# Key-major attention of one Trainium2 kernel: the turn of the maxima placed behind a two-head look in the memory stage, and the transfers of the rows of maxima issued by ScalarE instead of SyncE

## Time and profile before

| | |
|---|---|
| runs of the kernel before | 4800.02, 4809.53, 4809.84 us; median 4809.53 |
| the profiled execution | 4812.54 us |
| its span, first to last instruction | 4810.8 us, 75801 instructions |
| busy, share of the span | PE 80%, VectorE 71%, ScalarE 50%, GpSimd 30% |
| memory attention, looks and steps | about 3190 to 3575 us of the span |
| cross-self attention, looks and steps | about 3950 to 4665 us of the span |

### The profile page before, as it was taken

One profiled execution on the slowest core, in us unless ns is written; L12 is line 12 of the kernel. 1 busy time (PEld: TensorE's weight loads), 2 busy tenths in 40 slices (PEclk: granted clock), 3 DMA queues, 4 the chain that ended last, 5 costly groups with the idle time before them and its releaser, 6 DMA issues. The chain is left out here.

```text
span 4810.8 us, 75801 instructions
## 1 busy us (share of the span) xinstructions
PE 3834.0 (80%) x28914; PEld 2206.9 (46%) x28979; DVE 3405.1 (71%) x5269; ACT 2397.4 (50%) x3237; POOL 1425.0 (30%) x1078
## 2 busy tenths in 40 slices
PE   4740988999999999999984838849985858888883
PEld 3630445666666666666652514424433422222231
DVE  6469675878777877878774246667754658888868
ACT  2120224666666666666652125526652437767772
POOL 0000432666666666666663250000000000000000
PEclk5565998999999999999995659969986869999996
DMA  0010840000000000000002164145520433323300
GB/s 20 1 55 0 191 117 28 1 15 15 1 15 1 15 1 15 1 15 1 1 1 97 39 158 56 30 77 84 85 36 22 94 77 51 50 42 53 50 2 9
DMA packets 155463, 194.79 MB, mean 40 GB/s; under 512 B 23685, under 2 KB 117502, under 8 KB 154468
## 3 DMA queue, kind: packets, MB, share of 16 engines
q1 hardware_dynamic: 144068, 167.17, 17.3%
q0 software_dynamic: 9856, 22.67, 1.8%
q10 hardware_dynamic: 1184, 0.12, 0.0%
HBM read 145.03 MB, written 42.42 MB: 39 GB/s over the span
## 5 line engine op out<-in xcount | busy, mean ns | idle before, releaser
L3121 POOL TENSOR_TENSOR arena<-arena 128x512 f32<-128x512 f32 (+1 forms) x768 | 1133.2, 1477 | 629.9 <-ACT arena L3075 575.7
L2568 ACT ACTIVATE arena<-ps 128x1024 f32<-128x1024 f32 (+1 forms) x688 | 703.2, 1023 | 332.5 <-PE ps L2493 321.9
L2586 DVE TENSOR_REDUCE arena<-ps 128x2 f32<-128x826 f32 (+1 forms) x576 | 564.8, 981 | 182.2 <-PE ps L2439 173.9
L3137 DVE TENSOR_TENSOR arena<-arena 128x1024 f32<-128x1024 f32 (+1 forms) x448 | 653.2, 1497 | 34.9 <-ACT arena L3104 34.9
L3159 DVE TENSOR_TENSOR arena<-ps,arena 128x512 f32<-128x512 f32 (+1 forms) x768 | 530.3, 691 | 108.8 <-ACT arena L3069 75.3
L2439 PE MATMUL ps<-arena 48*128 48x413 bf16 (+3 forms) x1920 | 437.0, 334 | 133.8 <-DVE arena L2586 66.8
L3069 ACT ACTIVATE arena<-ps 128x1024 f32<-128x1024 f32 (+1 forms) x448 | 410.5, 960 | 200.6 <-PE ps L2997 194.8
L3075 ACT ACTIVATE arena<-arena 128x1024 f32<-128x1024 f32 (+1 forms) x448 | 425.0, 992 | 60.4 <-DVE arena L3137 57.9
L2512 PE MATMUL ps<-arena 128*9 128x256 f32 (+2 forms) x5504 | 437.1, 390 | 10.3 <-ACT arena L2556 7.5
L2997 PE MATMUL ps<-arena 64*128 64x256 f32 (+1 forms) x3328 | 427.4, 391 | 5.9 <-ACT arena L3091 1.3
L3011 PE MATMUL ps<-arena 128*64 128x256 f32 (+1 forms) x3328 | 411.1, 387 | 6.4 <-ACT arena L3075 6.4
(11 more groups left out here) (661 smaller groups left out, 5357.4 us busy)
## 6 DMA issues: line engine op xcount, KB each, us to landing
arena<-ctx_parts SPq DMA_DIRECT2D x96, 200.1 KB
arena<-ctx_parts SPq DMA_DIRECT2D x192, 100.1 KB
arena<-fs_rows SPq DMA_DIRECT2D x128, 128.0 KB, 6.7
arena<-in_ctx_feat SPq DMA_DIRECT2D x8, 1601.0 KB, 6.4
arena<-in_ctx SPq DMA_DIRECT2D x16, 768.0 KB
arena<-diff_att_stack SPq DMA_DIRECT2D x60, 192.0 KB, 6.6
ctx_parts<-arena SPq DMA_DIRECT2D x24, 400.2 KB, 7.4
arena<-in_ctx_feat SPq DMA_DIRECT2D x8, 800.5 KB, 9.3
```

The lines of the kernel that those rows point to most:

```text
L2568: act.activation(self.prob[0:rows, u % 3, :], self.ps[0:rows, 2 * (u % 2):2 * (u % 2) + 2, :].rearrange("p n c -> p (n c)"), ACT.Exp).then ...
L2586: ins = dve.tensor_reduce(dst[:, :, j // 2], self.ps[:, 4:6, 0:hi - lo], AX.X, ALU.max)
L3121: pool.tensor_tensor(acc[0:rows, u % 2, :], before, sc[0:rows, u % 2, t, :], ALU.add).then_inc(added, 1)
L3137: dve.tensor_tensor(e, e, mb[0:rows, u % 2, None, :].to_broadcast([rows, n, 2 * S]), ALU.subtract).then_inc(sub_done, 1)
```

## The change

It does three things.

1. For one lane (memory), `pair_from` takes the next even look at or after the count of looks at which the turn stood, and TensorE's turn follows that look, wherever in a step it falls; likewise the back, from the count at its step's middle. ScalarE's `act_rows` moves to the step in which that look is issued (`look_step`), behind its exponential. VectorE's `dve_out` follows the look of the back. Where no such look is left, and for two lanes (cross-self) always, turns and backs stay where they were (`late_turns`, `late_backs`).
2. ScalarE issues the transfers of the rows itself, at the end of `act_rows`, after a wait for its own copy.
3. SP only waits for the rows, and goes on with the unit's loads.

```diff
+        pair_from = lambda n: n + n % 2 if lanes == 1 else total
+        turn_look = {g: pair_from(self.looks_by(2 * self.turn_step(g) + 2)) for g in range(1, self.groups)}
+        back_look = {g: pair_from(self.looks_by(2 * self.back_step(g) + 1)) for g in range(self.groups - 1)}
+        self.turn_at = {n: g for g, n in turn_look.items() if n < total}
+        self.back_at = {n: g for g, n in back_look.items() if n < total}
+        self.rows_at = {self.look_step(n): g for n, g in self.turn_at.items()}
...
+    def look_step(self, n):
+
+        return next(u for u in range(self.groups * self.steps) if self.looks_by(2 * u + 2) > n)
...
-    def sp_rows(self, sp, g):
         s = self.sem
-        sp.wait_ge(s["rows_ready"], g + 1)
-        per, n = 24 // self.lanes, 4 // self.lanes
-        for e in range(self.lanes):
-            r0 = self.base(e) + self.rows
-            sp.dma_start(self.qst[r0:r0 + PARTS, self.unit(g) % 4, self.slot(g, 0):self.slot(g, 0) + n, :],
-                         self.max_rows[e * per:(e + 1) * per, :]).then_inc(s["max_loaded"], 16)
...
-            self.sp_rows(sp, g)
+            sp.wait_ge(s["rows_ready"], g + 1)
...
+        def look(n):
+            self.pe_look(pe, n)
+            if n in self.turn_at:
+                self.pe_turn_max(pe, self.turn_at[n])
+            if n in self.back_at:
+                self.pe_back(pe, self.back_at[n])
...
         act.activation(self.max_rows[0:24, :], self.ps[0:24, 7, 0:P], ACT.Copy).then_inc(s["rows_ready"], 1)
+        act.wait_ge(s["rows_ready"], g + 1)
+        per, n = 24 // self.lanes, 4 // self.lanes
+        for e in range(self.lanes):
+            r0 = self.base(e) + self.rows
+            act.dma_start(self.qst[r0:r0 + PARTS, self.unit(g) % 4, self.slot(g, 0):self.slot(g, 0) + n, :],
+                          self.max_rows[e * per:(e + 1) * per, :]).then_inc(s["max_loaded"], 16)
...
-            if u in turns:
-                self.act_rows(act, turns[u])
+            if u in self.rows_at:
+                self.act_rows(act, self.rows_at[u])
+            if u in self.late_turns:
+                self.act_rows(act, self.late_turns[u])
```

More of the change, by code:

```diff
@@ L2342, in __init__ @@
         self.ident_h = st.sb("ident_h", [P, P], BF16)
+        total = self.groups * self.looks
+        pair_from = lambda n: n + n % 2 if lanes == 1 else total
[4 more added lines that the diff above has]
+        self.rows_at = {self.look_step(n): g for n, g in self.turn_at.items()}
+        self.late_turns = {self.turn_step(g): g for g, n in turn_look.items() if n >= total}
+        self.late_backs = {self.back_step(g): g for g, n in back_look.items() if n >= total}
     def base(self, h):
@@ L2364, in turn_step, with back_step @@
         return g * self.steps - self.lead * self.steps // self.looks + 2
+    def look_step(self, n):
+        return next(u for u in range(self.groups * self.steps) if self.looks_by(2 * u + 2) > n)
+    def back_step(self, g):
+        return (g + 1) * self.steps + 2
     def run_pool(self, pool, spans):
@@ L2405, in sp_unit, with run_sp @@
             values(b)
-    def sp_rows(self, sp, g):
+    def run_sp(self, sp, stacks, values):
         s = self.sem
-        sp.wait_ge(s["rows_ready"], g + 1)
-        per, n = 24 // self.lanes, 4 // self.lanes
-        for e in range(self.lanes):
-            r0 = self.base(e) + self.rows
-            sp.dma_start(self.qst[r0:r0 + PARTS, self.unit(g) % 4, self.slot(g, 0):self.slot(g, 0) + n, :],
-                         self.max_rows[e * per:(e + 1) * per, :]).then_inc(s["max_loaded"], 16)
-    def run_sp(self, sp, stacks, values):
         self.sp_unit(sp, 1, stacks, values)
         for g in range(self.groups):
-            self.sp_rows(sp, g)
+            sp.wait_ge(s["rows_ready"], g + 1)
             w = self.unit(g) + 2
@@ L2518, in run_pe @@
         total = self.groups * self.steps
-        turns = {self.turn_step(g): g for g in range(1, self.groups)}
-        backs = {(g + 1) * self.steps + 2: g for g in range(self.groups - 1)}
         self.turned = self.backed = 0
         pe.wait_ge(self.sem["ones_loaded"], 4 * 2 * 16)
+        def look(n):
[4 more added lines that the diff above has]
+                self.pe_back(pe, self.back_at[n])
         for n in range(self.looks):
-            self.pe_look(pe, n)
+            look(n)
         self.pe_turn_max(pe, 0)
         for n in range(self.looks, self.looks_by(0)):
-            self.pe_look(pe, n)
+            look(n)
         for u in range(total):
@@ L2534, in run_pe @@
             for n in range(self.looks_by(2 * u + 1), self.looks_by(2 * u + 2)):
-                self.pe_look(pe, n)
-            if u in turns:
-                self.pe_turn_max(pe, turns[u])
-            if u in backs:
-                self.pe_back(pe, backs[u])
+                look(n)
+            if u in self.late_turns:
+                self.pe_turn_max(pe, self.late_turns[u])
+            if u in self.late_backs:
+                self.pe_back(pe, self.late_backs[u])
         self.pe_values(pe, total - 1)
@@ L2635, in look @@
                 self.dve_split(dve, link, n // self.looks)
+            if n in self.back_at:
+                self.dve_out(dve, link, self.back_at[n])
         for n in range(self.looks_by(0)):
@@ L2640, in run_dve @@
                 look(n)
-            if u in backs:
-                self.dve_out(dve, link, backs[u])
+            if u in self.late_backs:
+                self.dve_out(dve, link, self.late_backs[u])
         self.dve_out(dve, link, self.groups - 1)
```

## The result

The changed kernel takes **4904.67 us**, median of 4 runs (4862.62 to 4912.48), against 4804.9 us for the kernel before (4 runs, 4800.02 to 4809.84): a ratio of **1.0192**, 95% interval 1.0159 to 1.0225 (the ratio on record; the quotient of these two medians is 1.0208). It is slower, as forecast, but by some ten times the +10 us of the sum, and far outside the range of 4793 to 4839. The profiled execution took 4912.48 us, its span is 4910.5 us.

What follows compares the result with a forecast made beforehand. TensorE and VectorE, handing work to each other, were taken as the bound, with room on ScalarE on average. -6.4 + 0.7 + 31.0 - 15.2 = +10.1 us on the median of 4809.53 gave 4820 us, range 4793 to 4839.

Steps and rivals of the forecast that it cites:

- Part 1: Memory: the turn moves from behind look 29 to behind look 30, gaining 0.46 us on 14 turns, -6.4 us.
- Part 2: Memory: ScalarE's one transfer a turn fits before its next exponential; 0.72 us charged in group 15 only, +0.7 us.
- rival C: Memory: rows land 0.84 us late, the unit's loads starting beside them; 11.8 us over 14 turns, 4832; chance 0.09.
- Part 3: Memory: the back still follows look 64, and VectorE's division likewise stays; nothing.
- Part 4: Cross-self: two issues on ScalarE delay the next exponential 1.44 us, the values 1.0; over 31 turns +31.0 us.
- Part 5: Cross-self: five groups' late rows leave SP's queue, where the first stood 1.81 us; -15.2 us.
- Part 6: SP is freed of 0.72 and 1.44 us a group; nothing else waits for its loads; nothing.
- A: Cross-self, between copy and next exponential: issue short or not in ScalarE's way; 4803, or 4788 at no cost; chance 0.30.
- B: ScalarE and SP exclude each other while issuing, in cross-self's even groups and SP's value loads; 18.5 us, 4838; chance 0.11.
- D: Cross-self: nothing of the 15.2 us for late rows comes back; 4835; chance 0.05.

Runs made afterwards that it cites:

- kernel 1: The changed kernel with SP issuing the rows again in both stages, so only memory's moved turn is left; 4796.68 us, ratio 0.9978.
- both fillers: The changed kernel with matmuls nobody reads on TensorE in cross-self, in the turn's stall and ahead of even groups' scores; 4870.36 us, ratio 1.0135.
- kernel 3: The changed kernel, ScalarE still issuing, but SP holds a unit's loads until the rows have landed; 4844.35 us, ratio 1.0078.
- kernel 2: The changed kernel with SP issuing the rows in memory and ScalarE in cross-self alone; 4881.91 us, ratio 1.0159.

## Why the prediction was wrong

The sign was right and a good part of the mechanism, but the sum missed two terms: what the loads do to the rows once they start together, and the clock. Cross-self, kernel 1 to the changed kernel, 694.3 to 777.2 = +82.9 in the profiled executions: stalls 33.5 (31 x 1.08), the lower clock 40.4 (what both fillers give back; 34.3 in the medians), and a remainder of 9.0 for rows that land later than kernel 1's.

- **Part 1, memory's turn, -6.4.** Right. The period fell by 0.53 where 0.46 was worked out: 14 x 0.53 = 7.4. The 14 waits of the turn for VectorE (10.0 us) are gone; the wait of look 31 is put down to VectorE and not to the copy, which ended at nearly the same time. The whole gain was 13.4; the other 6 are long groups that went as well (last section).
- **Part 2, memory's issue on ScalarE, +0.7.** Right about ScalarE: the issue is hidden. Wrong as the price of the edit, about 23 us. What the step left out is rival C, chance 0.09: its 11.8 us is what the waits came to (11.3 us, 13 times), and the groups lost as much again. The step that failed is the argument against C: "at memory's turn the DMA engines are empty, and the packets are moved by 3358.75, 1.5 us from issue". That row was taken with the rows ahead of the loads on SP. Alone, the rows still land in 1.88 us (kernel 3); with loads started at the same moment they take 4.5.
- **Part 3, memory's back, nothing.** Nothing in kernel 1's plain groups speaks against it.
- **Part 4, the stall, +31.0.** Right: two issues of 0.75, 1.04 us idle, the period up by 1.08, 33.5 over 31 turns. The slack of 0.50 holds in two runs. But the step priced the stall by its length alone.
- **Part 5, the late rows, -15.2.** The odd groups did come back: 22.6 us, a plain group, in kernel 2. The forecast stopped there. Twelve even groups became late, 19.1 us of waits in place of 9.1.
- **Part 6, SP, nothing.** This is the step that failed first. "Its loads are two units ahead, and nothing else waits for them" looks at who waits for the loads. It doesn't ask what the loads now run beside. Freed of the rows, SP starts up to 4.43 us of issuing 0.03 us behind ScalarE. Kernel 3, which only moves that start, gives back 60 us of the median (4904.67 to 4844.35).
- **The clock.** The forecast priced it in part 5, for five groups, and in no other part. Idle time that the change adds has to be priced with what follows it: 40 us in cross-self, more than the stalls.

Of the rivals, A is out (the issue is 0.75 us, over the 0.56 from which it decides). B is out: ScalarE's pair takes 1.49 us with SP quiet and 1.52 beside SP's twelve. C was the one, in both stages, though it named memory alone. D is out for the groups that it spoke of. The rule of the Trainium skill on which D leaned ("DMA: Bandwidth & Descriptors", section "Issuing engines are not separate DMA queues") was set aside too soon: the packets of the two queues do share the engines (242 beside the 30), and the even groups paid for it, group 8 with 9.4 us in place of 2.65, while the odd ones did gain the sequencer's time.

## What to carry to other kernels

An order on one queue can be worth more than a second queue: a small transfer that is needed soon lands quickest when it is issued ahead of the large ones, or when these wait until it has landed. When a step is moved off a queue, ask what that queue does earlier for it. And when a change adds idle time to TensorE, price the clock behind it as well as the wait; matmuls that compute nothing, put into the idle time, measure that share.

## What the runs showed that was not expected

**The clock falls behind waits of about a microsecond.** TensorE busy 0.16 us of 1.00, then 13 us at 0.51, as shown above; in kernel 3 a group at 0.93 behind a stall of 1.04 us; and matmuls that compute nothing took 34 us off the median.

**GpSimd's repack of the values stretches VectorE's small operations.** The changed kernel, in the timeline of memory:

```profile
3278.01 1.74 POOL L2404 COPY arena<-arena 128x1536 f32<-128x1536 f32 x2 [50.52 <-DMA arena<-in_ctx]
3278.21 1.32 DVE L2630 TENSOR_TENSOR arena<-arena 128x8 bf16<-128x8 f32 x1
```

And the same statement in kernel 1, all 16 groups of memory (ns: least, median, most):

```profile
L2633 DVE TENSOR_TENSOR arena<-arena x16: 166/168/169, 3217.3 to 3547.5; 128x8 bf16<-128x8 f32 x16
```

An operation of 0.17 us takes 1.32 when it meets the repack, and the turn needs its result. One of the four small operations by which VectorE splits the maxima is stretched so (1.10 to 1.48 us) six times in memory after, three times before, and never in kernel 1, where the repack falls a few microseconds later in the group (at 3286.01, 4.3 ahead of the copy, where it is 6.8 in the changed kernel). The three groups of the kernel before are three of its four long ones (23.68, 23.36 and 25.11 us). So part of memory's gain with the moved turn, and of its loss with the late rows, seems to be a meeting of two engines that no edit touched. The Trainium skill ("SBUF — State Buffer", section "SBUF: two separate sides") has such a lock between the two engines, held for a whole instruction; these rows agree. Whether these meetings account for all of the rest of memory's difference was not tried.
